# Destination logits spread by small transfers through device memory, q and k biases on ScalarE, new instruction lists

## The reference, cut to what matters

```python
def _L1_gnn_ref(x, adj, W, a_src, a_dst):
    Wh = jnp.einsum('bnd,de->bne', x, W)
    e_src = jnp.einsum('bnd,d->bn', Wh, a_src)
    e_dst = jnp.einsum('bnd,d->bn', Wh, a_dst)
    logits = e_src[:, :, None] + e_dst[:, None, :]
    logits = jnp.where(logits >= 0, logits, NEG_SLOPE * logits)
    logits = jnp.where(mask, -jnp.inf, logits)
    attn = jax.nn.softmax(logits, axis=-1)
    ...
    out = jnp.einsum('bnm,bmd->bnd', attn, Wh)
...
def _L3_gnn_ref(h, adj, Wq, bq, Wk, bk, Wv, bv, Wo, bo):
    q = split_heads(h @ Wq.T + bq)
    k = split_heads(h @ Wk.T + bk)
    v = split_heads(h @ Wv.T + bv)
    scores = jnp.einsum('bhqd,bhkd->bhqk', q, k) * scale
    ...
h = jnp.maximum(_layernorm(x, axis=-1), 0.0)
x = x + _L0_gnn_ref(h, adj, L0_gnn_W, L0_gnn_b)
...
x = x + _L3_gnn_ref(h, adj, ...)
```

## Time and profile before

| | |
|---|---|
| median of the runs | 1312.32 us |
| the profiled execution's own time | 1311.95 us |
| its span, first to last instruction | 1310.1 us |
| TensorE busy | 1268.5 us, 97% |
| VectorE busy | 1114.6 us, 85% |
| ScalarE busy | 1034.0 us, 79% |
| GpSimd busy | 927.3 us, 71% |
| mean granted TensorE clock | 0.995 |

### The profile page before, as it was taken

The page is one execution under the profiler, slowest core; times in us unless marked ns, Lnnn a source line. Parts: engine busy times, 40 slices in busy tenths (PEclk is TensorE's granted clock), DMA queues, the critical chain, the costliest instruction groups (busy, mean ns, idle before and its releaser), DMA issues. The chain is left out here.

```text
span 1310.1 us, 42658 instructions
## 1 busy us (share of the span) xinstructions
PE 1268.5 (97%) x12433; PEld 1158.5 (88%) x12433; DVE 1114.6 (85%) x5713; ACT 1034.0 (79%) x3907; POOL 927.3 (71%) x1232
## 2 busy tenths in 40 slices
PE   5899999999999999999999999999999999999985
PEld 4689999999999999999999999999999999999874
DVE  5788889889889888888888888888888988988863
ACT  2478888888888888788788888888888888888885
POOL 4777777777777777777777777777777777776652
PEclk9899999999999999999999999999999999999999
DMA  4001101100100100100100110110110110100000
GB/s 123 26 10 34 34 18 35 34 20 32 35 26 26 35 26 26 35 26 26 34 28 24 34 34 18 34 35 18 34 34 18 34 34 20 33 26 10 18 18 25
DMA packets 38899, 38.97 MB, mean 30 GB/s; under 512 B 3088, under 2 KB 38672, under 8 KB 38672
## 3 DMA queue, kind: packets, MB, share of 16 engines
q1 hardware_dynamic: 36608, 34.94, 8.7%
q10 hardware_dynamic: 2064, 1.32, 0.3%
HBM read 19.47 MB, written 16.78 MB: 28 GB/s over the span
## 5 line engine op out<-in xcount | busy, mean ns | idle before, releaser
L704 ACT ACTIVATE exps<-masked,nmax 128x128 f32<-128x128 f32 x1024 | 399.1, 408 | 2.2 <-POOL probs L308 2.2
L308 POOL TENSOR_TENSOR probs<-exps,rsum 128x512 f32<-128x512 f32 x256 | 267.1, 1044 | 154.7 <-DVE rsum L515 154.7
L279 POOL TENSOR_TENSOR rstd<-veps,power 128x2 f32<-128x2 f32 x256 | 178.6, 697 | 185.8 <-DVE veps L420 185.4
L287 POOL TENSOR_SCALAR y<-x,nm,rstd 128x256 f32<-128x256 f32 x512 | 282.0, 562 | 22.3 <-issue 20.9
L507 DVE CUSTOM_DVE_ANT_0 masked<-bank,mask 128x128 f32<-128x128 f32 x1024 | 227.4, 283 | 2.0 <-PE bank L906 2.0
L704 ACT ACTIVATION_READ_ACCUMULATOR exps<-masked,nmax 128x1 f32 x1024 | 211.4, 206 | 0.0
L800 PE MATMUL bank<-w_hi,ht_hi 128*128 128x512 f32 (+1 forms) x512 | 195.2, 381 | 7.2 <-DVE ht_lo L449 6.8
L404 DVE BATCH_NORM_STATS2 stats<-x 128x6 f32<-128x256 f32 x512 | 190.1, 413 | 6.5 <-DMA x<-in_x 4.2
L801 PE MATMUL bank<-w_lo,ht_hi 128*128 128x512 f32 (+1 forms) x512 | 176.2, 344 | 0.0
L802 PE MATMUL bank<-w_hi,ht_lo 128*128 128x512 f32 (+1 forms) x512 | 175.2, 342 | 0.0
L690 ACT ACTIVATE at<-bank 128x256 f32<-128x256 f32 x128 | 49.3, 385 | 143.3 <-PE bank L863 143.3
(11 more groups left out here) (116 smaller groups left out, 3703.7 us busy)
## 6 DMA issues: line engine op xcount, KB each, us to landing
x<-in_x SPq DMA_DIRECT2D x64, 256.0 KB, 2.7
out<-x SPq DMA_DIRECT2D x64, 256.0 KB, 2.1
probs<-in_w0t SPq DMA_DIRECT2D x1, 512.0 KB, 5.5
w_sb<-in_w ACTq DMA_DIRECT2D x1, 256.0 KB, 3.9
probs<-in_w1t ACTq DMA_DIRECT2D x1, 256.0 KB, 4.3
exps<-in_wot SPq DMA_DIRECT2D x1, 256.0 KB, 7.9
exps<-in_wkt ACTq DMA_DIRECT2D x1, 256.0 KB, 7.9
exps<-in_wqt SPq DMA_DIRECT2D x1, 256.0 KB, 8.7
```

Source lines behind the costliest of these rows:

```text
L279: pool.tensor_tensor(rstd[i][:, b], veps[i][:, b], power[:], ALU.pow).then_inc(S[f"rstd{i}"], 1)
L287: last = pool.tensor_scalar(y[i][:, b, g], src[:, bx, g], nm[i][:, s, g:g + 1], rstd[i][:, s, g:g + 1], ALU.add, ALU.mult)
L308: pool.tensor_tensor(probs3[:, p % BUFFERS["probs3"], j], exps3[:, p % BUFFERS["exps3"], j], rsum3[:, s, j].unsqueeze(2).to_broadcast([P, ...
L704: last = act.activation(exps3[:, b, j, i], masked3[:, p % BUFFERS["masked3"], j, i], ACT.Exp, bias=nmax3[:, s, j, i:i + 1], scale=-1.0, ac ...
```

## The change

The transposes `d1` and `d2` leave TensorE. In their place GpSimd copies the two destination numbers of each node (one for each graph of the pair) into a small tile `dst` of 128x2 (`gather_dst`). SyncE writes it to a device memory buffer of 1 KB, eight bytes from each partition (`write_row`), waits until that has landed, and reads the 1 KB back into all 128 partitions (`spread_row`, tile `db`, 128x256). ScalarE's `sum_logits` now reads `db` from SBUF, every second element, and writes a PSUM tile of its own (`zz1`, `zz2`, both in bank 7). Each transfer has two slots.

`add_bias` moves from VectorE to ScalarE (Identity with bias and scale). Since ScalarE multiplies before it adds, bq is multiplied by the scale once, at the start, on VectorE.

LAG, BANKS and the order within each engine's step are all new. TensorE's order becomes `pt2`, `h0t`, `pt3`, `x2_mm`, `h3t`, `ot_mm`, `s0`, `m0`, `qt_mm`, `kt_mm`, `x4_mm`, `h2t`, `scores`, `pt0`, `e2t`, `hh_mm`, `h1t`, `x3_mm`, `pt1`, `m1`, `v_mm`, `wh1_mm`, `wh0_mm`, `e1t`; its smallest LAG is -1 and its largest 6. ScalarE's becomes `p3t_1`, `exp1`, `wh1`, `wh0`, `at1`, `p3t_2`, `p3t_3`, `v`, `h0t_hi`, `h3t_hi`, `exp3_1`, `ot_hi`, `mj_hi0`, `exp3_0`, `z2`, `qt`, `kt`, `exp2`, `ht2`, `exp3_3`, `at2`, `p3t_0`, `hh`, `h1t_hi`, `z1`, `exp3_2`, `mj_hi1`. GpSimd's becomes `y1`, `r3`, `rstd0`, `dst2`, `p3_3`, `y0`, `rstd3`, `y3`, `dst1`, `p3_2`, `r0`, `x3_tail`, `p3_1`, `rstd2`, `y2`, `p3_0`, `rstd1`. VectorE's is new likewise. Buffers of the pipeline stay as they were.

The core of the diff (the lists of the steps and most of BANKS are left out; of LAG the new one is shown):

```diff
 LAG = {
+       "row_in2": 1, "row_out1": -1, "store": 6, "load": -5, "row_in1": -1, "row_out2": 0, "pt2": 6, "h0t": -1, "pt3": 6, "x2_mm": 2, "h3t": 4,
+       "ot_mm": 6, "s0": 0, "m0": -1, "qt_mm": 4, "kt_mm": 4, "x4_mm": 6, "h2t": 2, "scores": 4, "pt0": 5, "e2t": 3, "hh_mm": 2, "h1t": 0, "x3_mm": 3,
+       "pt1": 5, "m1": -1, "v_mm": 4, "wh1_mm": 0, "wh0_mm": 0, "e1t": 1, "p3t_1": 6, "exp1": 2, "wh1": 1, "wh0": 1, "at1": 2, "p3t_2": 6, "p3t_3": 6,
+       "v": 5, "h0t_hi": -1, "h3t_hi": 4, "exp3_1": 5, "ot_hi": 6, "mj_hi0": -1, "exp3_0": 5, "z2": 3, "qt": 4, "kt": 4, "exp2": 3, "ht2": 2,
+       "exp3_3": 5, "at2": 3, "p3t_0": 5, "hh": 2, "h1t_hi": 0, "z1": 1, "exp3_2": 4, "mj_hi1": -1, "mj_lo1": 0, "veps3": 4, "nmax3_3": 5,
+       "rsum1_any": 2, "t0_1": 0, "nmax3_0": 5, "rsum1": 2, "h0t_lo": -1, "x2": 2, "h3t_lo": 4, "stats2": 2, "rsum3_1": 5, "mv2": 2, "veps2": 2,
+       "x1": 0, "ot_lo": 6, "stats1": 0, "nmax2": 3, "mv1": 0, "rsum3_0": 5, "veps1": 0, "mv0": -2, "veps0": -2, "t0_0": -1, "mj_lo0": -1,
+       "stats0": -3, "x4": 6, "rsum2": 3, "nmax3_2": 4, "rsum3_3": 5, "nmax3_1": 4, "x3": 3, "h1t_lo": 0, "nmax1": 1, "stats3": 3, "rsum3_2": 4,
+       "mv3": 3, "y1": 1, "r3": 5, "rstd0": -1, "dst2": 3, "p3_3": 6, "y0": -1, "rstd3": 4, "y3": 4, "dst1": 1, "p3_2": 5, "r0": -2, "x3_tail": 3,
+       "p3_1": 5, "rstd2": 2, "y2": 2, "p3_0": 5, "rstd1": 0,
...
+    "zz2": (7, "z2", ('nmax2',)),
+    "zz1": (7, "z1", ('nmax1',)),
...
+        db = [None] + [sb(f"db{i}", [P, 2, G * P]) for i in (1, 2)]
+        dst = [None] + [sb(f"dst{i}", [P, 2, G]) for i in (1, 2)]
+        rows = [None] + [nc.dram_tensor(f"rows{i}", [2, P, G], F32).ap() for i in (1, 2)]
+        row_out = [None] + [[sem(f"row{i}_out{b}") for b in range(2)] for i in (1, 2)]
+        row_in = [None] + [[sem(f"row{i}_in{b}") for b in range(2)] for i in (1, 2)]
...
+            def write_row(i, p):
+                b = p % 2
+                passed(sp, f"dst{i}", p)
+                if p >= 2:
+                    sp.wait_ge(row_in[i][b], p // 2 * 16)
+                sp.dma_start(rows[i][b], dst[i][:, b]).then_inc(row_out[i][b], 16)
+
+            def spread_row(i, p):
+                b = p % 2
+                sp.wait_ge(row_out[i][b], (p // 2 + 1) * 16)
+                passed(sp, f"z{i}", p, 2)
+                sp.dma_start(db[i][:, b], rows[i][b].rearrange("n g -> (n g)").partition_broadcast(P)).then_inc(row_in[i][b], 16)
+
             def step(t):
+                if due(t, "row_in2"):
+                    spread_row(2, t - LAG["row_in2"])
+                if due(t, "row_out1"):
+                    write_row(1, t - LAG["row_out1"])
+                if due(t, "store"):
+                    store(t - LAG["store"])
                 if due(t, "load") and t - LAG["load"] >= 2:
                     load(t - LAG["load"])
-                if due(t, "store"):
-                    store(t - LAG["store"])
+                if due(t, "row_in1"):
+                    spread_row(1, t - LAG["row_in1"])
+                if due(t, "row_out2"):
+                    write_row(2, t - LAG["row_out2"])
...
+            def gather_dst(i, src, buffer, ready, col, p):
+                b, bs = p % 2, p % BUFFERS[buffer]
+                passed(pool, ready, p)
+                if p >= 2:
+                    pool.wait_ge(row_out[i][b], p // 2 * 16)
+                pool.tensor_copy(dst[i][:, b], src[:, bs, :, col]).then_inc(S[f"dst{i}"], 1)
...
+                dve.wait_ge(wq_in, 32)
+                dve.tensor_scalar(bq_sb[:], bq_sb[:], float(DH) ** -0.5, None, ALU.mult)
...
-                    last = dve.tensor_tensor_reduce(z[i][:, b, g], bank_of(f"d{i}")[:, (G + g) * P:(G + g + 1) * P], msk[:], scale=-1.0, scalar=-MASKED, op0=ALU.add, op1=ALU.min,
+                    last = dve.tensor_tensor_reduce(z[i][:, b, g], bank_of(f"zz{i}")[:, g * P:(g + 1) * P], msk[:], scale=-1.0, scalar=-MASKED, op0=ALU.add, op1=ALU.min,
...
-            def add_bias(name, dst, bias, scale, p):
-                b = p % BUFFERS[name]
-                passed(dve, f"{name}_mm", p)
-                read_before(dve, name, p, "scores")
-                for c in range(DC):
-                    last = dve.tensor_scalar(dst[:, b, c], bank_of(name)[:, c * G * P:(c + 1) * G * P], bias[:, c:c + 1], scale, ALU.add, ALU.mult)
-                last.then_inc(S[name], 1)
...
             def sum_logits(i, src, buffer, col, p):
                 bs = p % BUFFERS[buffer]
-                passed(act, f"d{i}", p)
-                for g in range(G):
-                    last = act.activation(bank_of(f"d{i}")[:, (G + g) * P:(G + g + 1) * P], bank_of(f"d{i}")[:, g * P:(g + 1) * P], ACT.Prelu, bias=src[:, bs, g, col:col + 1], alpha=SLOPE)
+                act.wait_ge(row_in[i][p % 2], (p // 2 + 1) * 16)
+                bank_free(act, f"zz{i}", p)
+                for g in range(G):
+                    last = act.activation(bank_of(f"zz{i}")[:, g * P:(g + 1) * P], db[i][:, p % 2].rearrange("p (n g) -> p g n", g=G)[:, g], ACT.Prelu, bias=src[:, bs, g, col:col + 1], alpha=SLOPE)
                 last.then_inc(S[f"z{i}"], 1)
...
+            def add_bias(name, dst, bias, scale, p):
+                b = p % BUFFERS[name]
+                passed(act, f"{name}_mm", p)
+                read_before(act, name, p, "scores")
+                for c in range(DC):
+                    last = act.activation(dst[:, b, c], bank_of(name)[:, c * G * P:(c + 1) * G * P], ACT.Identity, bias=bias[:, c:c + 1], scale=scale)
+                last.then_inc(S[name], 1)
...
-                if due(t, "d1"):
-                    spread_dst(1, wh, "wh", last_of("wh0", "wh1"), D + 1, t - LAG["d1"])
...
-                if due(t, "d2"):
-                    spread_dst(2, hh, "hh", "hh", F1 + 1, t - LAG["d2"])
```

More of the change, by code:

```diff
@@ L29 @@
 LAG = {
[9 rows of a table removed]
[10 rows of a table added]
 }
 BANKS = {
-    "m1": (4, "m1", ('mj_lo1', 't0_1')),
-    "pt3": (2, "pt3", ('p3t_3',)),
-    "v": (0, "v_mm", ('v',)),
-    "ot": (3, "ot_mm", ('ot_lo',)),
[L47 to L63, removed]
-    "sc1": (1, "scores", ('nmax3_1',)),
[L65 to L71, removed]
+    "pt2": (1, "pt2", ('p3t_2',)),
+    "h0t": (2, "h0t", ('h0t_lo',)),
+    "pt3": (3, "pt3", ('p3t_3',)),
+    "x2b": (0, "x2_mm", ('x2',)),
+    "h3t": (1, "h3t", ('h3t_lo',)),
+    "ot": (3, "ot_mm", ('ot_lo',)),
+    "x1b": (5, "s0", ('x1',)),
+    "m0": (6, "m0", ('mj_lo0', 't0_0')),
+    "qt": (4, "qt_mm", ('qt',)),
+    "kt": (1, "kt_mm", ('kt',)),
+    "x4b": (0, "x4_mm", ('x4',)),
+    "h2t": (3, "h2t", ('ht2',)),
+    "sc0": (4, "scores", ('nmax3_0',)),
+    "sc1": (1, "scores", ('nmax3_1',)),
+    "sc2": (5, "scores", ('nmax3_2',)),
+    "sc3": (2, "scores", ('nmax3_3',)),
+    "pt0": (3, "pt0", ('p3t_0',)),
+    "at2": (6, "e2t", ('at2',)),
+    "hh": (0, "hh_mm", ('hh',)),
+    "h1t": (6, "h1t", ('h1t_lo',)),
+    "x3b": (5, "x3_mm", ('x3',)),
+    "pt1": (0, "pt1", ('p3t_1',)),
+    "m1": (3, "m1", ('mj_lo1', 't0_1')),
+    "v": (5, "v_mm", ('v',)),
+    "wh1": (1, "wh1_mm", ('wh1',)),
+    "wh0": (6, "wh0_mm", ('wh0',)),
+    "at1": (0, "e1t", ('at1',)),
+    "zz2": (7, "z2", ('nmax2',)),
+    "zz1": (7, "z1", ('nmax1',)),
 }
@@ L179, in gnn_kernel @@
         x_out = [sem(f"x_out{i}") for i in range(BUFFERS["x4"])]
-        S = {name: sem(name) for name in LAG if name not in ("load", "store")}
+        S = {name: sem(name) for name in LAG if name not in ("row_in2", "row_out1", "store", "load", "row_in1", "row_out2")}
         for name in ("nm0", "nm1", "nm2", "nm3",):
@@ L317, in step @@
             def step(t):
+                if due(t, "y1"):
+                    normalise(1, x1, t - LAG["y1"])
+                if due(t, "r3"):
+                    biased_x3(t - LAG["r3"])
+                if due(t, "rstd0"):
+                    inverse_deviation(0, t - LAG["rstd0"])
+                if due(t, "dst2"):
+                    gather_dst(2, hh, "hh", "hh", F1 + 1, t - LAG["dst2"])
+                if due(t, "p3_3"):
+                    normalise_p3(3, t - LAG["p3_3"])
+                if due(t, "y0"):
+                    normalise(0, x0, t - LAG["y0"])
+                if due(t, "rstd3"):
+                    inverse_deviation(3, t - LAG["rstd3"])
+                if due(t, "y3"):
+                    normalise(3, x3, t - LAG["y3"])
+                if due(t, "dst1"):
+                    gather_dst(1, wh, "wh", last_of("wh0", "wh1"), D + 1, t - LAG["dst1"])
+                if due(t, "p3_2"):
+                    normalise_p3(2, t - LAG["p3_2"])
                 if due(t, "r0"):
@@ new lines, in step @@
+                if due(t, "x1"):
+                    sum_x1(t - LAG["x1"])
+                if due(t, "ot_lo"):
+                    low_ot(t - LAG["ot_lo"])
+                if due(t, "stats1"):
+                    stats_of(1, x1, t - LAG["stats1"])
+                if due(t, "nmax2"):
+                    mask_logits(2, mask2, t - LAG["nmax2"])
+                if due(t, "mv1"):
```

(41 more changed lines are left out.)

272 lines of the change are left out of this document (107 added, 165 removed), and 9 rows, old and new, of the table LAG.

## The result

The changed kernel takes 1329.26 us (median of 4 runs, 1328.37 to 1330.99), the kernel before 1312.03 in the same measurement: a ratio of 1.0136, with a 95% interval from 1.0118 to 1.0153. It is slower by 17 us, and 38 us above the 1291 that were predicted. Its profiled span is 1327.4 us. Of the kernels further down, one execution of the kernel with the bias on VectorE took 3995 us where its other three took 1420 to 1421; its ratio leaves that one out.

The account below looks back on a forecast made before the run. The prediction took TensorE's instructions, start to start, as the bound: 64 steps of 19.06 us are 1219.8, plus 69 for the ramps and 2.2 from span to median, gives 1291 us, range 1281 to 1303.

Parts of the forecast that it names:

- Removed from TensorE, 0.44 us a step: TensorE's steady step: two pairs of transposes go, about 0.22 us each, so 19.06 us a step and 28 us in all.
- ScalarE at 17.8 us a step, covered: ScalarE's step grows from 16.07 us by the moved biases and SBUF reads, bounds 17.1 to 18.6, staying below 19.06.
- GpSimd at 14.7: GpSimd's step with two added 128x2 copies of 0.2 us each: 14.7 us, at most 15.7, covered by TensorE.
- VectorE loses four instructions ... 15.5 of 19.06: VectorE's step loses four bias instructions of 0.44 us, 1.75 together, leaving 15.5 us busy; that alone saves nothing.
- The check of what TensorE waits for: In the new order's layout, the tightest slacks, at x2_mm, ot, pt1 and h1t: 0.4 to 0.7 us, positive.
- sign of being wrong: In the steady part: steps of 19.3 us or longer would show the prediction wrong, against 19.0 to 19.1 expected.
- its other two: Further signs of a wrong prediction: ScalarE waits for a DMA in every step, or ramps grow past 80 us.
- The ramps at 69 us: Start and end of the run: 69 us beside the 64 steps, up from 62.1, between 62.1 and 72.5.
- the first, lists that don't keep TensorE full: Late copies in the steps: part of gain left, 1301 to 1309.7, chance 0.11; none left 0.05; more lost 0.02.
- The slow transfers: Small transfers land slowly and ScalarE stands before z1: 2.3 us a step longer, 147 us, so 1438; chance 0.08.
- the 8 and 6 us to spare: Slack between the spread destination row's arrival and its use: 8 us before z1, 6 us before layer 2's z2.
- ScalarE did not become the bound: Rival for ScalarE's step: 3.0 us more, as by function table reloads for Identity, would give over 1400; chance 0.02.

Follow-up runs that it names:

- e2t: Not a run: a block of TensorE's step order, right ahead of hh_mm; it needs PSUM bank 6 from mj_lo0, with some 0.5 us to spare.
- both reductions: The changed kernel with VectorE's two small instructions veps and nm written as reductions instead of TENSOR_SCALAR, lists untouched: 1290.1 us, ratio 0.9828.
- veps moved: The changed kernel with veps2 moved behind ot_lo and veps0 behind mj_lo0 in VectorE's list, nothing else changed: 1293.3 us, ratio 0.9856.

## Why the prediction was wrong

- **Removed from TensorE, 0.44 us a step:** right. 0.43 by putting them back, and steps of 19.01 wherever TensorE is full.
- **ScalarE at 17.8 us a step, covered:** right, 17.92. **GpSimd at 14.7:** right, 14.65, its copies 0.19 each.
- **"VectorE loses four instructions ... 15.5 of 19.06":** this is the step that failed. It was 16.78. The four instructions did go; without the holds VectorE has 15.7, the other 0.2 being that the four take 0.39 each from start to start (in the kernel before, qt's two from 708.49 to 709.28) and not 0.44. What I took over unseen was the 0.16 us of veps, which takes 0.90 and 0.76 at two of its four places. It is the duration under the old lists, where veps rarely stood beside a GpSimd instruction; the new lists put two of four beside the multiplications of 1.04 us. A new list changes not only when an instruction starts but how long it takes. The sum priced every instruction by its mean of before, and the lists were laid out for what waits for what, not for what runs beside what. The prediction took VectorE for covered because it is busy for less than a step. At 16.78 it still is; what counted was one stretch of it, the 9 us without a gap from h0t_lo to x4.
- **The check of what TensorE waits for** named four tight places of 0.4 to 0.7 us and left out the one that gave way, hh_mm behind x4. It put x4 at about 10 us of the step; it began at 12.1 (714.18, the step's first transpose being at 702.04). Of these 2.1 us the holds are 0.74 + 0.60, the rest an error of the layout that would have done no harm: in the kernel with both reductions x4 starts 7.3 us after s0, instead of 8.4, and it ends at 729.17 while hh_mm starts at 729.75; hh_mm follows the end of x4 by 0.15 where it waits for it, so 0.4 us are to spare. With the holds hh_mm starts 0.90 us after e2t (714.10 to 715.00) and without them 0.22 (729.53 to 729.75): that is 0.68 of the 0.71 by which the step grew, of which the profile calls 0.52 a wait. The prediction's own sign of being wrong, steps of 19.3 or longer, came true; its other two did not.
- **The ramps at 69 us:** 65 in the changed kernel, 77 in the one with veps moved (1293.8 - 64 x 19.01, with a granted clock of 0.91 in the first 100 us), 70 with both reductions. The size was right. For the reason, that transfers lengthen the chain, the runs give no clear answer: the changed kernel without them has 1328.9 - 64 x 19.73 = 66, no less than with them, but the one with veps moved and the numbers spread by TensorE has 1313.7 - 64 x 19.44 = 70, less than 77.
- **Rivals:** the first, lists that don't keep TensorE full, is what happened, and it took more than the whole gain, for which it had 0.02. The slow transfers did not: writing lands in 3.1 us and reading in 3.8, where the sum had 2.1 and 2.7; of the 8 and 6 us to spare 2 are used. The Trainium skill's rule on small writes, which the prediction set beside it, did not decide anything here. ScalarE did not become the bound, at 17.92, and its function table is still loaded only once.

The Trainium skill has the rule that I should have weighed against the new order (SBUF — State Buffer, SBUF: two separate sides): VectorE and GpSimd share one pair of ports, which is locked for a whole instruction, by a VectorE instruction in a mode that uses two ports or, where GpSimd's instruction reads SBUF, with two SBUF inputs, and the loser waits. The traces agree with it for TENSOR_SCALAR from SBUF to SBUF, held to within 0.03 us of the end of GpSimd's instruction, and for the reduction, which is not held; in which mode the TENSOR_SCALAR ran, no view shows. They agree for an instruction with two SBUF inputs too. The product of rsum and has_any stands right ahead of VectorE's idle time in each step, and it meets the start of a multiplication in 5 of the changed kernel's 64 pairs. There it takes 1.02 to 1.07 us, where its mean in the kernel before is 0.16, and the idle time behind it takes that up:

```profile
347.23 1.06 DVE L512 TENSOR_TENSOR rsum<-rsum,has_any 128x2 f32<-128x2 f32 x1
```
```profile
347.24 1.04 POOL L342 TENSOR_TENSOR probs<-exps,rsum 128x512 f32<-128x512 f32 x1
```

## What to carry to other kernels

When instruction lists are redrawn, don't price the small SBUF instructions of VectorE by their old means: lay VectorE's and GpSimd's lists side by side, and keep TENSOR_SCALAR, and what reads two tiles of SBUF, off GpSimd's long instructions in the stretches that TensorE waits for, by moving it or by giving it another form. A mean far above that of its twin (475 beside 158 ns) is the sign, since neither the busy share nor the waits show a hold. And where an engine waits for another with which it shares no data, look at the table of PSUM banks.
